# The router's logits of a fusion layer: weight columns as the stationary side of TensorE's products, or 128 tokens

## The chip, the core and the metric

The kernel runs on one core of a Trainium2 chip. A time is the device time of one execution in microseconds (us). TensorE (PE) multiplies, VectorE (DVE), ScalarE (ACT) and GpSimd (POOL) work elementwise, SyncE (SP) starts transfers. A TensorE product has a stationary side, which is loaded first (a record of its own, PEld), and a moving side, whose columns then stream past it; the result stands in PSUM with the stationary side's columns as its partitions and the moving side's columns as its elements.

## The reference, cut to what matters

Images are cut into patches and embedded, joined with text to 16 sequences of 69 tokens (1104 tokens of 256 values), and pass one attention layer. Then comes a mixture of experts; the router is the part that changes:

```
h = h + attention(layernorm(h))
x = layernorm(h)                                  # 1104 tokens x 256
shared = expert(x, shared_up, shared_down)        # every token, gelu(x @ up) @ down
probs = softmax(x @ router_w)                     # router_w: 256 x 8 experts
top_k_prob, top_k_idx = top_k(probs, 2)
out = h + shared + x + sum over the 2 experts of prob * expert(x)
```

## The kernel before, in words

Every engine has its own list of instructions, written out by hand in one block; they meet at semaphores. There is no scheduler: the order in the code is the order on the engine.

After attention the normalized tokens stand transposed in `hT_n` as two parts, a rounded high part and the low rest (fp32r each; a product of two such numbers is three products: high x high, high x low, low x high, `split_product`). `flat_transposes(g)` turns group g of 276 tokens (four sequences) into PSUM, ACT writes the high part (`flat_high`), DVE the low part (`flat_low`, semaphore `f_lo`).

The shared expert goes over all tokens in 24 steps n: three blocks of SN = 384 tokens times eight slices of 128 hidden values. `shared_up(n)` is six products of 384 columns, ACT takes the gelu twice (`shared_act`, `s_act`), DVE writes the low part (`shared_parts`, `s_lo`), `shared_down(n)` is nine products of 256 columns. `shared_up(n)` waits until `s_lo` has reached n - 1, that is until DVE has taken step n - 2.

Between these steps the router is woven in. TPAD = 1152 padded tokens are NT = 9 tiles of 128 or NSG = 3 blocks of 384; NE = 8 experts, KD = 2 slices of the 256 inputs. `router(q)` makes the logits of block q as 8 partitions x 384 in PSUM bank 7, ACT copies them to `lturn` (`logits_copy`), and when all three are there `router_turn` turns them tile by tile, so that tokens are partitions. All three blocks use the same piece of bank 7, so `router(1)` and `router(2)` wait for the copy before them. DVE then takes the maximum and subtracts it (`r_sub`), ACT takes the exponential, for which it loads another table and afterwards the gelu's again, and DVE goes on with a long chain of small operations (top two, ranks, places), at the end of which stands the table `dest` that says which rows belong to which expert tile. Its parts alternate on DVE with `shared_parts`, so that a late chain holds up the shared expert's steps: `shared_parts(6, 7)` stands behind the softmax's sum and product.

After the shared expert TensorE runs 25 expert tiles in a loop, GpSimd gathers rows, splits expert weights and adds the results to the output.

The line numbers of before that the rows use: L978 to L980 are `split_product` (router, shared_up, experts), L853 every transpose, L1028 `shared_down`, L774 `logits_copy`, L804 the exponential, L723 `flat_high`, L716 `flat_base`, L768 and L769 `shared_act`, L1370 `shared_parts`, L1378 `shared_end`, L1412 and L1413 the maximum and the subtraction, L1091 the sums over tiles that give ranks.

Of the kernel before, what the change touches and what calls it, by code (L numbers as in the profile page):

```python
# [13 lines left out]
P = 128  # L14
# [52 lines left out]
def fusion_layer(nc, patches, txt, cls_token, cls_pos, ln1_gb, tok_w, tok_bias, ln2_g, ln2_b,  # L67
# [5 lines left out]
    def sb(name, shape, dt=F32, where=ctx, side="left"):  # L73
        return where.enter_context(nc.sbuf_tensor(name, shape, dt, side=side))

    def sem(name):
        return ctx.enter_context(nc.semaphore(name))
# [5 lines left out]
    with ctx:  # L83
# [15 lines left out]
        additions = sb("additions", [1, TILES], I32)  # L99
        tend_int = sb("tend_int", [1, NE], I32)  # L100
        rw = sb("rw", [P, KD, NE])
        rws = sb("rws", [P, 2, KD, NE], F32R)
        st2 = sb("st2", [SEQ, NG, GB, 6])
        mv2 = sb("mv2", [SEQ, NG, GB, 2])
        rs2 = sb("rs2", [SEQ, NG, GB])
# [64 lines left out]
        slots12.close()  # L170

        sb("slots12", [P, 4 * EW], where=early)
        turned = ExitStack()
        lturn = sb("lturn", [NE, TPAD], where=turned)
        turned.close()
        in_lane = sb("in_lane", [P, 2 * NT, P], where=early)
        above = sb("above", [P, 2 * NT, TILES], where=early)
        in_tile = sb("in_tile", [P, 2 * NT, TILES], where=early)
# [45 lines left out]
        f_stats, f_rstd, f_normed, f_base, f_tr, f_hi, f_lo = (  # L224
            sem(n) for n in ("f_stats", "f_rstd", "f_normed", "f_base", "f_tr", "f_hi", "f_lo"))
        pads, rws_ready, logits = sem("pads"), sem("rws_ready"), sem("logits")
        l_turned, l_taken = sem("l_turned"), sem("l_taken")
        r_sub, r_exp, r_mask, r_prefix, r_tiles = (
            sem(n) for n in ("r_sub", "r_exp", "r_mask", "r_prefix", "r_tiles"))
        r_told, r_table_mm, r_table = sem("r_told"), sem("r_table_mm"), sem("r_table")  # L230
# [411 lines left out]
        def _(act):  # L642
# [126 lines left out]
                    nc.scalar.activation(up, up, ACT.Gelu).then_inc(s_act, 1)  # L769


            def logits_copy(q):
                act.wait_ge(l_turned, q + 1)
                nc.scalar.activation(lturn[:, SN * q:SN * (q + 1)], ps[0:NE, 7, 0:SN], ACT.Copy).then_inc(l_taken, 1)  # L774

            def expert_high(n):

                part, k = n // 4, n % 4
# [11 lines left out]
            flat_norm(2)  # L790
            shared_act(2, 3)
            flat_high(2)
            logits_copy(0)
            shared_act(3, 4)
            flat_norm(3)
            shared_act(4, 5)
# [1 line left out]
            shared_act(5, 6)  # L798
            flat_base(2)
            shared_act(6, 7)  # L800
            logits_copy(1)
            logits_copy(2)
            act.wait_ge(r_sub, 1)
            nc.scalar.activation(rout[:, 1, :], rout[:, 0, :], ACT.Exp).then_inc(r_exp, 1)  # L804
            shared_act(7, 8)
# [45 lines left out]
        def _(te):  # L851
            def transpose(o, i, n):
                return nc.tensor.transpose(o, i, ident[0:n, 0:n])  # L853
# [98 lines left out]
            def flat_transposes(g):  # L952
                te.wait_ge(f_normed, g + 1)
                te.wait_ge(a_rope, min(g + 3, NG))
                if g == 1:
                    te.wait_ge(f_lo, 1)
                elif g >= 2:
                    te.wait_ge(a_pTs, NG)
                    if g == 3:
                        te.wait_ge(f_lo, 3)  # L960
                for c in range(KD):
                    for b in range(GB):
                        last = transpose(flat_ps(g, c)[:, SEQ * b:SEQ * (b + 1)], hn2[:, g % 2, b, P * c:P * (c + 1)], SEQ)
                last.then_inc(f_tr, 1)
# [10 lines left out]
            def split_product(o, pairs):  # L975

                for n, (a, b) in enumerate(pairs):
                    nc.tensor.matmul(o, a[0], b[0], start=n == 0, stop=False)  # L978
                    nc.tensor.matmul(o, a[0], b[1], start=False, stop=False)  # L979
                    last = nc.tensor.matmul(o, a[1], b[0], start=False, stop=n == len(pairs) - 1)  # L980
                return last

            def router(q):

                te.wait_ge(a_exp, NG)
                te.wait_ge(rws_ready, 1)
                te.wait_ge(f_lo, GROUPS_OF[q])
                if q >= 1:
                    te.wait_ge(l_taken, q)
                split_product(ps[0:NE, 7, 0:SN],  # L990
                              [([rws[:, v, c, :] for v in range(2)],
                                [hT_n[:, v, c, SN * q:SN * (q + 1)] for v in range(2)])
                               for c in range(KD)]).then_inc(l_turned, 1)

            def router_turn():
                te.wait_ge(l_taken, NSG)
                for i in range(NT):
                    last = transpose(ps[:, 7, SN + NE * i:SN + NE * (i + 1)], lturn[:, P * i:P * (i + 1)], NE)
                last.then_inc(logits, 1)

            def shared_up(n0, n1):

# [29 lines left out]
            def shared_steps(n0, n1):  # L1032
                for n in range(n0, n1):
                    shared_up(n, n + 1)
                    shared_down(n - LAG, n - LAG + 1)
# [37 lines left out]
            attention_out(NG - 1)  # L1073
            shared_up(2, 4)
            flat_transposes(2)
            router(0)
            shared_down(0, 1)
            shared_steps(4, 6)
            flat_transposes(3)
            shared_steps(6, 7)  # L1080
            te.wait_ge(pads, 1)
            router(1)
            router(2)
            router_turn()
            shared_steps(7, 10)

            te.wait_ge(r_mask, 1)
# [76 lines left out]
        def _(dve):  # L1164
# [196 lines left out]
            v.tensor_scalar(token[:, :], small[:, S_TOK:S_TOK + NT], -float(T + P), None, ALU.add)  # L1361

            dve.wait_ge(router_in, 16)
            link(v.tensor_copy(rws[:, 0, :, :], rw[:, :, :]))
            v.tensor_tensor(rws[:, 1, :, :], rw[:, :, :], rws[:, 0, :, :].bitcast(F32), ALU.subtract).then_inc(rws_ready, 1)

            def shared_parts(n0, n1):
                for n in range(n0, n1):
# [39 lines left out]
            over_e = lambda a: a.unsqueeze(2).to_broadcast([P, NT, NE])  # L1408
            rank = small[:, S_RANK:S_RANK + NE].unsqueeze(1).to_broadcast([P, NT, NE])
            dve.wait_ge(logits, 1)  # L1410
            lg = n3(ps[:, 7, SN:SN + NT * NE])
            link(v.tensor_reduce(rsm[:, 0, :], lg, AX.X, ALU.max))  # L1412
            v.tensor_tensor(n3(rout[:, 0, :]), lg, over_e(rsm[:, 0, :]), ALU.subtract).then_inc(r_sub, 1)  # L1413
            dve.wait_ge(r_exp, 1)
            link(v.tensor_reduce(rsm[:, 1, :], n3(rout[:, 1, :]), AX.X, ALU.add))
            link(v.reciprocal(rsm[:, 2, :], rsm[:, 1, :]))
# [196 lines left out]
```

## Time and profile before

| | |
|---|---|
| median of 3 runs | 341.75 us (339.48 to 342.25) |
| the profiled execution's time | 340.2 us |
| its span in the profile | 338.4 us |
| mean granted TensorE clock | 0.984 of full speed |
| busy: PE, PEld, DVE, ACT, POOL | 89%, 80%, 47%, 43%, 62% |
| router, first product of block 0 to DVE's maximum | 92.72 to 107.17 us |
| shared expert's last product, expert tiles | to about 157 us, then to 330 us |

Times of single rows are microseconds from the span's start. A busy share says how long an engine had something in it, not that it set the end; the waits say that.

### The profile page before, as it was taken

How to read it: one execution, taken by the hardware profiler on the slowest of the kernel's cores; microseconds unless marked ns; L12 is line 12 of the kernel's file. 1: busy time of each engine (PE TensorE's matmuls, PEld its weight loads, DVE VectorE, ACT ScalarE, POOL GpSimd, SP SyncE). 2: the span in 40 equal slices, each digit the busy share in tenths (PEclk: the TensorE clock that was granted, in tenths of full speed). 3: DMA queues.
4: the chain of work that ended last, by engine and by line, in shares of the span. 5: the costliest groups of instructions: out<-in, count | busy, mean ns of one | idle time of the engine just before them, and what ended most of it. 6: DMA issues, size and time to landing. Idle time of an engine off the chain costs nothing.

```text
span 338.4 us, 6655 instructions
## 1 busy us (share of the span) xinstructions
PE 301.1 (89%) x2049; PEld 269.5 (80%) x2050; DVE 159.8 (47%) x402; ACT 145.3 (43%) x327; POOL 210.0 (62%) x168
## 2 busy tenths in 40 slices
PE   0879788998897969999899999999999999999970
PEld 0456587887795969998699989998999899899960
DVE  3558867888853399473223332433233233323220
ACT  2647313375978533642444344333433343344210
POOL 2476373148882000755988988898888899335551
PEclk9997979999999999999999999999999999999997
DMA  7955404002464230375453364255333633224522
GB/s 235 314 104 158 144 26 158 0 27 63 153 211 157 97 119 2 108 239 193 164 169 108 137 201 163 52 172 186 114 111 101 175 57 47 34 44 47 64 33 31
DMA packets 21926, 39.91 MB, mean 118 GB/s; under 512 B 2914, under 2 KB 18227, under 8 KB 19603
## 3 DMA queue, kind: packets, MB, share of 16 engines
q0 software_dynamic: 7456, 25.43, 28.0%
q1 hardware_dynamic: 14162, 14.03, 13.4%
q10 hardware_dynamic: 288, 0.20, 0.2%
q8 instruction: 11, 0.18, 0.2%
q14 instruction: 9, 0.07, 0.1%
HBM read 28.84 MB, written 6.93 MB: 106 GB/s over the span
## 4 chain that ended last, share of the span: by engine, by line
PE 41%; POOL 12%; DMA 12%; issue 8%; DVE 7%; ACT 2%; POOLq 2%; SPq 0%; DVEq 0%; ACTq 0%
DMA out_tokens<-xy_all,dest 11%; PE ps L978 9%; PE ps L979 9%; PE ps L980 9%; PE ps L1028 7%; POOL ring L443 6%; PE ps L853 4%; POOL ring L442 3%; POOL out_tokens L590 2%; PE ps L948 2%; POOLq L587 1%; PE ps L1100 1%; DVE h L1286 1%; DVE ps L1258 1%; DVE qk L1257 1%
## 5 line engine op out<-in xcount | busy, mean ns | idle before, releaser
L443 POOL TENSOR_TENSOR ring<-stage,ring 128x512 fp32r<-128x512 f32 (+2 forms) x30 | 76.2, 2541 | 2.5
L1549 DVE TENSOR_TENSOR hgT<-ps,hgT 128x512 fp32r<-128x512 f32 x50 | 32.2, 687 | 72.2 <-ACT hgT L843 72.2
L978 PE MATMUL ps<-ring,hgT 128*128 x200 | 58.0, 290 | 2.1 <-DVE xy_all L1555 1.5
L590 POOL DMA_INDIRECT out_tokens<-xy_all,dest x25 | 39.5, 1582 | 27.5 <-DMA out_tokens<-xy_all,dest 15.6
L980 PE MATMUL ps<-ring,hgT 128*128 x200 | 55.9, 279 | 0.0
L979 PE MATMUL ps<-ring,hgT 128*128 x200 | 55.9, 279 | 0.0
L835 ACT ACTIVATE hg<-ps 128x512 f32<-128x512 f32 x50 | 29.9, 599 | 47.6 <-PE ps L980 47.6
L580 POOL DMA_INDIRECT xy_all<-normalized_tokens,dest x25 | 24.9, 997 | 38.8 <-DVE dest L1511 31.4
L978 PE MATMUL ps<-ring,xgT 128*128 x100 | 41.3, 413 | 1.1 <-issue 0.6
L442 POOL TENSOR_SCALAR ring<-stage 128x512 fp32r<-128x512 f32 (+2 forms) x30 | 38.5, 1284 | 2.6 <-PEq L1114 2.4
L978 PEld LDWEIGHTS ps<-ring,hgT 128*128 128x128 f32 x200 | 37.6, 188 | 2.6 <-issue 2.6
L979 PE MATMUL ps<-ring,xgT 128*128 x100 | 39.4, 394 | 0.0
L980 PE MATMUL ps<-ring,xgT 128*128 x100 | 39.2, 392 | 0.0
L979 PEld LDWEIGHTS ps<-ring,hgT 128*128 128x128 f32 x200 | 37.7, 188 | 0.0
L980 PEld LDWEIGHTS ps<-ring,hgT 128*128 128x128 f32 x200 | 37.6, 188 | 0.0
L818 ACT ACTIVATE xgT<-ps 128x256 fp32r<-128x256 f32 x25 | 9.6, 386 | 53.7 <-PE ps L853 53.7
L1555 DVE TENSOR_SCALAR xy_all<-ps,gate 128x256 f32 (+1 forms) x25 | 12.1, 484 | 38.6 <-PE ps L980 38.6
L1028 PE MATMUL ps<-ring,hid 128*128 128x256 f32 x216 | 29.5, 282 | 0.2 <-DVE base L1378 0.2
L1028 PEld LDWEIGHTS ps<-ring,hid 128*128 128x128 f32 x216 | 28.3, 189 | 0.6 <-issue 0.5
L843 ACT ACTIVATE hgT<-ps 128x512 fp32r<-128x512 f32 x50 | 27.1, 599 | 2.6 <-PE ps L853 2.6
L853 PE MATMUL ps<-mats,hg 128*128 128x128 f32 x200 | 25.9, 272 | 0.0
L853 PEld LDWEIGHTS ps<-mats,hg 128*128 128x128 f32 x200 | 23.3, 140 | 3.2
(193 smaller groups left out, 591.0 us busy)
## 6 DMA issues: line engine op xcount, KB each, us to landing
stage<-in_w_up POOLq DMA_DIRECT2D x9, 1024.0 KB, 5.5
stage<-in_w_dn POOLq DMA_DIRECT2D x9, 1024.0 KB, 5.6
xg<-xy_all SPq DMA_DIRECT2D x25, 128.0 KB, 2.7
xp<-in_patches SPq DMA_DIRECT2D x4, 384.0 KB, 7.6
normalized_tokens<-hn SPq DMA_DIRECT2D x4, 276.0 KB
residual_tokens<-h SPq DMA_DIRECT2D x4, 276.0 KB
ring<-in_tok_w SPq DMA_DIRECT2D x1, 768.0 KB, 7.0
base<-residual_tokens SPq DMA_DIRECT2D x2, 384.0 KB, 4.1
```

The costliest lines, as they stand in the source:

```text
L442: link(nc.gpsimd.tensor_scalar(hi, stage[:, part, c0:c1], 1.0, 0.0, ALU.mult, ALU.add))
L443: return nc.gpsimd.tensor_tensor(lo, stage[:, part, c0:c1], hi.bitcast(F32), ALU.subtract)
L580: pool.indirect_dma_start(xy_all[:, t, :], None, xn_d, bass.IndirectOffsetOnAxis(ap=dest[:, t:t + 1].bitcast(U32), axis=0)).then_inc(rows_ ...
L590: pool.indirect_dma_start(out, bass.IndirectOffsetOnAxis(ap=dest[:, t:t + 1].bitcast(U32), axis=0), xy_all[:, t, :], None, compute_op=ALU. ...
L835: nc.scalar.activation(hg[:, 1 - c, 512 * half:512 * (half + 1)], ps[:, hidden_bank + half, :], ACT.Gelu).then_inc(e_act, 1)
L843: nc.scalar.activation(hgT[:, c, 0, 4 * half:4 * half + 4, :], ps[:, turned_bank + half, :].rearrange("p (k t) -> p k t", k=4), ACT.Copy). ...
L853: return nc.tensor.transpose(o, i, ident[0:n, 0:n])
L978: nc.tensor.matmul(o, a[0], b[0], start=n == 0, stop=False)
L979: nc.tensor.matmul(o, a[0], b[1], start=False, stop=False)
L980: last = nc.tensor.matmul(o, a[1], b[0], start=False, stop=n == len(pairs) - 1)
L1028: last = nc.tensor.matmul(ps[:, down_bank[j], 0:D], a[x], b[y], start=f == 0 and m == 0, stop=f == KF - 1 and m == 2)
L1549: v.tensor_tensor(hgT[:, c, 1, 4 * half:4 * half + 4, :], ps[:, turned_bank + half, :].rearrange("p (k t) -> p k t", k=4), hgT[:, c, 0, 4 ...
```

## The change

The router's products change sides. 128 tokens of `hT_n` are the stationary side and the router's weights the moving one: for each tile of 128 tokens and each of the two slices, the high part of the tokens meets 16 columns (8 of the weights' high part and 8 of their low part, which `rws` now holds side by side), and the low part of the tokens meets the 8 high columns and is added onto the first 8. The logits then have tokens as partitions at once: each tile has 16 values of its own in bank 7, the three copies on ACT, the nine turns on TensorE, `lturn` and the two semaphores between them are gone. DVE adds the two halves: it copies the second to `rout` and adds the first, and then takes the maximum and subtracts from there.

The products are also placed otherwise. Before, block 0 (384 tokens) stood after `flat_transposes(2)` and blocks 1 and 2 together after step 6. Now tiles 0 to 3 (512 tokens) stand after `flat_transposes(2)`, tiles 4 and 5 after `flat_transposes(3)`, and tiles 6 to 8 after step 6.

```diff
-        rws = sb("rws", [P, 2, KD, NE], F32R)
+        rws = sb("rws", [P, KD, 2, NE], F32R)
...
-            def logits_copy(q):
-                act.wait_ge(l_turned, q + 1)
-                nc.scalar.activation(lturn[:, SN * q:SN * (q + 1)], ps[0:NE, 7, 0:SN], ACT.Copy).then_inc(l_taken, 1)
...
             flat_high(2)
-            logits_copy(0)
             shared_act(3, 4)
...
             shared_act(6, 7)
-            logits_copy(1)
-            logits_copy(2)
             act.wait_ge(r_sub, 1)
...
-            def router(q):
+            def logits_of(i):
+                return ps[:, 7, 2 * NE * i:2 * NE * (i + 1)]
+
+            def router(i0, i1):
 
                 te.wait_ge(a_exp, NG)
                 te.wait_ge(rws_ready, 1)
-                te.wait_ge(f_lo, GROUPS_OF[q])
-                if q >= 1:
-                    te.wait_ge(l_taken, q)
-                split_product(ps[0:NE, 7, 0:SN],
-                              [([rws[:, v, c, :] for v in range(2)],
-                                [hT_n[:, v, c, SN * q:SN * (q + 1)] for v in range(2)])
-                               for c in range(KD)]).then_inc(l_turned, 1)
-
-            def router_turn():
-                te.wait_ge(l_taken, NSG)
-                for i in range(NT):
-                    last = transpose(ps[:, 7, SN + NE * i:SN + NE * (i + 1)], lturn[:, P * i:P * (i + 1)], NE)
-                last.then_inc(logits, 1)
+                te.wait_ge(f_lo, -(-min(P * i1, T) // GT))
+                for i in range(i0, i1):
+                    for c in range(KD):
+                        high, low = (hT_n[:, n, c, P * i:P * (i + 1)] for n in range(2))
+                        nc.tensor.matmul(logits_of(i), high, rws[:, c, :, :].rearrange("p v e -> p (v e)"), start=c == 0,
+                                         stop=False)
+                        last = nc.tensor.matmul(logits_of(i)[:, 0:NE], low, rws[:, c, 0, :], start=False, stop=c == KD - 1)
+                if i1 == NT:
+                    last.then_inc(logits, 1)
...
             flat_transposes(2)
-            router(0)
+            router(0, 4)
             shared_down(0, 1)
             shared_steps(4, 6)
             flat_transposes(3)
+            router(4, 6)
             shared_steps(6, 7)
             te.wait_ge(pads, 1)
-            router(1)
-            router(2)
-            router_turn()
+            router(6, NT)
             shared_steps(7, 10)
...
-            lg = n3(ps[:, 7, SN:SN + NT * NE])
-            link(v.tensor_reduce(rsm[:, 0, :], lg, AX.X, ALU.max))
-            v.tensor_tensor(n3(rout[:, 0, :]), lg, over_e(rsm[:, 0, :]), ALU.subtract).then_inc(r_sub, 1)
+            lg = ps[:, 7, 0:2 * NT * NE].rearrange("p (n v e) -> p n v e", v=2, e=NE)
+            link(v.tensor_copy(n3(rout[:, 1, :]), lg[:, :, 1, :]))
+            link(v.tensor_tensor(n3(rout[:, 0, :]), lg[:, :, 0, :], n3(rout[:, 1, :]), ALU.add))
+            link(v.tensor_reduce(rsm[:, 0, :], n3(rout[:, 0, :]), AX.X, ALU.max))
+            v.tensor_tensor(n3(rout[:, 0, :]), n3(rout[:, 0, :]), over_e(rsm[:, 0, :]), ALU.subtract).then_inc(r_sub, 1)
```

What stands on TensorE from `flat_transposes(3)` (the `hn` row) to `shared_up(7)` before; the `ring` rows are a shared step's products, the `rws` rows the router's. Left out are the rest of step 6 and of the router's twelve products:

```order
L853 MATMUL ps<-mats,hn 128x69 x8
L978 MATMUL ps<-hT_n,ring 128x384
...
L1028 MATMUL ps<-ring,hid 128x256 x9
L978 MATMUL ps<-hT_n,rws 8x384
L979 MATMUL ps<-hT_n,rws 8x384
L980 MATMUL ps<-hT_n,rws 8x384
...
L853 MATMUL ps<-mats,lturn 128x8 x9
L978 MATMUL ps<-hT_n,ring 128x384
```

And in the changed kernel, at the same place:

```order
L842 MATMUL ps<-mats,hn 128x69 x8
L983 MATMUL ps<-rws,hT_n 128x16
L985 MATMUL ps<-rws,hT_n 128x8
...
L967 MATMUL ps<-hT_n,ring 128x384
...
L1016 MATMUL ps<-ring,hid 128x256 x9
L983 MATMUL ps<-rws,hT_n 128x16
L985 MATMUL ps<-rws,hT_n 128x8
...
L967 MATMUL ps<-hT_n,ring 128x384
```

Eight short products now stand ahead of step 6 and twelve behind it, where twelve long ones and nine turns stood behind it.

On ACT, from `flat_high(3)` to the exponential, before:

```order
L723 ACTIVATE hT_n<-ps 128x276 x2
L768 ACTIVATE hid<-ps 128x384
L769 ACTIVATE ps<-ps 128x384
L716 ACTIVATE h<-h,nb,sp 69x256 x4
L768 ACTIVATE hid<-ps 128x384
L769 ACTIVATE ps<-ps 128x384
L774 ACTIVATE lturn<-ps 8x384 x2
L804 ACT_TABLE_LOAD
L804 ACTIVATE rout<-rout 128x72
```

And in the changed kernel:

```order
L719 ACTIVATE hT_n<-ps 128x276 x2
L764 ACTIVATE hid<-ps 128x384
L765 ACTIVATE ps<-ps 128x384
L712 ACTIVATE h<-h,nb,sp 69x256 x4
L764 ACTIVATE hid<-ps 128x384
L765 ACTIVATE ps<-ps 128x384
L793 ACT_TABLE_LOAD
L793 ACTIVATE rout<-rout 128x72
```

The two copies between the gelu of step 6 and the table load are gone; nothing else moved on ACT but the first copy, further up.

## Rows read from the trace of the kernel before

**Rows 1.** The page: busy time, share of the span and instructions of each engine.

```profile
PE 301.1 (89%) x2049; PEld 269.5 (80%) x2050; DVE 159.8 (47%) x402; ACT 145.3 (43%) x327; POOL 210.0 (62%) x168
```

**Rows 2.** The chain that ended last, in order of time: start us, us, what.

```profile
101.41 1.97 ACT h L716 x4
...
104.12 0.40 ACT lturn L774
...
118.93 0.75 DVE base L1378 x2
...
160.58 1.98 DMA xg<-xy_all
```

**Rows 3.** Timeline, 92 to 95 us: start us, us, engine line op [idle before <-releaser].

```profile
92.72 0.37 PE L978 MATMUL ps<-hT_n,rws 128*8 128x384 f32 x1
...
93.81 1.22 PE L1028 MATMUL ps<-ring,hid 128*128 128x256 f32 x9
...
94.25 0.55 DVE L1370 TENSOR_TENSOR hid<-ps,hid 128x384 fp32r<-128x384 f32 x1
...
94.94 0.42 PE L978 MATMUL ps<-hT_n,ring 128*128 128x384 f32 x1
```

**Rows 4.** Timeline, 99 to 107 us.

```profile
99.24 0.67 PE L853 MATMUL ps<-mats,hn 69*128 69x69 f32 x8
...
99.75 0.42 PE L978 MATMUL ps<-hT_n,ring 128*128 128x384 f32 x1
...
99.94 0.70 ACT L723 ACTIVATE hT_n<-ps 128x276 fp32r<-128x276 f32 x2 [0.93 <-PE ps L853]
...
100.88 1.23 PE L1028 MATMUL ps<-ring,hid 128*128 128x256 f32 x9
...
101.94 0.34 PE L978 MATMUL ps<-hT_n,rws 128*8 128x384 f32 x1
...
104.04 0.46 ACT L774 ACTIVATE lturn<-ps 8x384 f32<-8x384 f32 x1
...
104.65 0.33 PE L978 MATMUL ps<-hT_n,rws 128*8 128x384 f32 x1 [1.50 <-ACT lturn L774]
...
105.88 0.48 ACT L774 ACTIVATE lturn<-ps 8x384 f32<-8x384 f32 x1 [1.38 <-PE ps L980]
106.38 1.28 ACT L804 ACT_TABLE_LOAD   x1
```

**Rows 5.** Timeline, 107 to 110 us.

```profile
107.06 0.45 PE L978 MATMUL ps<-hT_n,ring 128*128 128x384 f32 x1
...
107.17 0.23 DVE L1412 TENSOR_REDUCE rsm<-ps 128x9 f32<-128x72 f32 x1 [5.18 <-PE ps L853]
...
107.44 0.23 DVE L1413 TENSOR_TENSOR rout<-ps,rsm 128x72 f32<-128x72 f32 x1
...
107.71 0.26 ACT L804 ACTIVATE rout<-rout 128x72 f32<-128x72 f32 x1
...
108.78 0.56 DVE L1370 TENSOR_TENSOR hid<-ps,hid 128x384 fp32r<-128x384 f32 x1
...
109.48 0.42 PE L978 MATMUL ps<-hT_n,ring 128*128 128x384 f32 x1
```

**Rows 6.** Weight loads in the timeline from 113.5 us.

```profile
113.93 2.09 PEld L1091 LDWEIGHTS ps<-rsel,mats 128*128 128x128 f32 x18
115.94 0.30 PEld L1094 LDWEIGHTS ps<-mats 128*128 128x128 f32 x2
```

**Rows 7.** One tile's instructions (lturn): ns min/median/max, first and last start us.

```profile
L853 PEld LDWEIGHTS ps<-mats,lturn x9: 133/137/138, 106.4 to 106.9; 8*128 8x128 f32 x9
L853 PE MATMUL ps<-mats,lturn x9: 200/201/223, 106.4 to 106.9; 8*128 8x8 f32 x9
```

**Rows 8.** GpSimd's timeline from 112 us.

```profile
135.97 1.07 POOL L580 DMA_INDIRECT xy_all<-normalized_tokens,dest  x1 [31.41 <-DVE dest L1511]
...
330.78 1.56 POOL L590 DMA_INDIRECT out_tokens<-xy_all,dest  x1 [1.17 <-DVE xy_all L1555]
```

More of the change, by code:

```diff
@@ L172, in fusion_layer @@
         sb("slots12", [P, 4 * EW], where=early)
-        turned = ExitStack()
-        lturn = sb("lturn", [NE, TPAD], where=turned)
-        turned.close()
         in_lane = sb("in_lane", [P, 2 * NT, P], where=early)
@@ L226, in fusion_layer @@
         pads, rws_ready, logits = sem("pads"), sem("rws_ready"), sem("logits")
-        l_turned, l_taken = sem("l_turned"), sem("l_taken")
         r_sub, r_exp, r_mask, r_prefix, r_tiles = (
@@ L1363, in _ @@
             dve.wait_ge(router_in, 16)
-            link(v.tensor_copy(rws[:, 0, :, :], rw[:, :, :]))
-            v.tensor_tensor(rws[:, 1, :, :], rw[:, :, :], rws[:, 0, :, :].bitcast(F32), ALU.subtract).then_inc(rws_ready, 1)
+            link(v.tensor_copy(rws[:, :, 0, :], rw[:, :, :]))
+            v.tensor_tensor(rws[:, :, 1, :], rw[:, :, :], rws[:, :, 0, :].bitcast(F32), ALU.subtract).then_inc(rws_ready, 1)
             def shared_parts(n0, n1):
```

## The prediction

> **What bounds the kernel now.** I began with the page: TensorE has something in it for 89% of the span, the others for 43 to 62% [rows 1]. That alone says little about the router, so I followed the chain of work that ended last through it [rows 2]. It is on TensorE nearly everywhere, but between 100 and 107 us it leaves it: it runs through ACT's `flat_base` and gelu and then through a copy to `lturn`. The reader is to see in [rows 4] that this is a ping-pong: copy of block 1 on ACT at 104.04, block 2's products on TensorE at 104.65 after 1.50 us of idleness, copy of block 2 on ACT at 105.88, and right behind it the load of the exponential's table, 1.28 us. DVE waits 5.18 us for the logits and starts at 107.17, the exponential at 107.71 [rows 5].
>
> Who waits for that? The shared step 6 on DVE stands behind the softmax; it runs from 108.78 to 109.34, and TensorE's `shared_up(8)` starts at 109.48, 0.14 us after it [rows 5]. From there the chain goes on through TensorE, DVE's `shared_end`, and the first rows for the expert tiles [rows 2]. GpSimd sits idle for 31.41 us until the table `dest` comes out of the same DVE chain, and its last addition waits for DVE's last result [rows 8]. I found nothing behind 109.48 that is due at a fixed time, so a shift there should reach the end whole.
>
> **What the change removes.** From the start of the first late copy to the start of the table load, 104.04 to 106.38, there are 2.34 us on ACT [rows 4]: two copies, block 2's products between them and the waits. All of it goes. The nine turns go too. The copy of block 0 lies in a stretch where ACT afterwards waits anyway; I count nothing for it.
>
> **What one new product costs.** It loads 128 columns and moves 16 or 8. No router product of before is like that: they load 8 columns and move 384, at 1.09 us for six with what lies around them (92.72 to 93.81) [rows 3]. The nearest row is L1091: 128 columns loaded, 8 to 72 moved, and 18 loads go from 113.93 to the next group's at 115.94, 2.01 us or 0.112 us each [rows 6]. The load sets this pace, since the moved columns change and the pace doesn't. The lower end is the nine turns of `lturn`, also 128 columns loaded and 8 moved, whose starts lie within 0.5 us, 0.064 us each [rows 7]. They are turns, though, and a load there lasts 137 ns where L1094's two take 0.30 us together [rows 6, 7]. I take 0.112.
>
> The Trainium skill, "TensorE: Matmul & The Clock Gate", section "Back-to-back issue gap", gives about 81 ns for a sustained pair of load and product at 128 columns. L1091 of this case doesn't agree, with 112 ns. By the page the delay ahead of `flat_transposes(3)` below would be 0.14 us and the gain 2.2 us, an estimate of 338.0 us for the profiled execution.
>
> **What the change adds, place by place.** Tiles 0 to 3 are 16 products, 1.79 us where 1.09 stood. `shared_down(0)` is nine products, 1.06 us (as from 100.88 to 101.94 [rows 4]), so it ends at 92.72 + 1.79 + 1.06 = 95.57. `shared_up(4)` starts at 94.94 now, just behind DVE's step 2 (94.25 + 0.55 = 94.80) [rows 3]. TensorE is therefore 0.63 us late there, and no wait up to `flat_transposes(3)` takes it back, as the two steps between run without a gap. So this delay is on the path: the turns start at 99.24 + 0.63 = 99.87, and ACT, which waits for them (0.93 us before L723 [rows 4]), is late by the same 0.63.
>
> On ACT the rest up to the table load is unbroken work: the load starts at 104.04 + 0.63 = 104.67 and ends at 105.95 instead of 107.66.
>
> On TensorE: 99.87 + 0.51 (the turns, 99.24 to 99.75) + 8 x 0.112 + 1.13 (`shared_up(6)`, 99.75 to 100.88) + 1.06 + 12 x 0.112 = 104.81 [rows 4, 6]. ACT's `flat_base` hides the 0.90 us of tiles 4 and 5 from ACT's path; without that cover they would cost it 0.90 more. With the last product's own length (0.20, as in [rows 7], less the pace) DVE can start at about 104.95.
>
> DVE has two more operations ahead of the maximum, a copy and an addition of 128 x 72. The two that are there follow each other by 0.27 us and last 0.23 each [rows 5]: four make 3 x 0.27 + 0.23 = 1.04 us, 0.54 more than now. The difference is ready at 104.95 + 1.04 = 105.99, where it was at 107.67. It comes within 0.04 us of the table load, so both paths give the same. The exponential starts at about 106.03 instead of 107.71: **1.7 us earlier**.
>
> What is late next? DVE's step 6 ends at 109.34 - 1.7 = 107.66, and `shared_up(8)` can start at 107.8. TensorE arrives at 104.81 + 1.13 + 1.06 = 107.0, so it stands idle for 0.8 us. `shared_up(7)` is 2.25 us earlier (107.06 to 104.81 [rows 5]), but 0.6 of that is given back here. Work added to TensorE on balance: 36 x 0.112 = 4.0 us against 18 products at 1.09 us for six and nine turns at 0.064, 3.9 us. It is the waiting that goes, not the work.
>
> **The sum.** The profiled execution's 340.2 us less 1.7 is 338.5. It lies 1.55 us under the median of the three runs; on that scale the forecast is 341.75 - 1.65 = **340.1 us**, half a per cent faster. The three runs spread over 2.8 us, so a change of less than about 1% is what a measurement of this kernel can hardly tell from none.
>
> **Rivals.**
>
> *The new products are cheap* (0.064 us, the turns' pace). Then tiles 0 to 3 take 1.02 us and delay nothing, the table load starts at 104.04, the exponential at 104.04 + 1.28 + 0.04 = 105.36, and the gain is 2.35 us: 339.4 on the median's scale. DVE would be ready before, so ACT's path sets it. For it speaks that the turns have the same columns on both sides, against it that they are no arithmetic. Were TensorE the bound behind the router, the gain would be 2.25 us, nearly the same; the 0.14 us between DVE's step 6 and `shared_up(8)` speaks against that.
>
> *The time is taken back later*: some transfer or GpSimd's additions set the rest, and nothing changes, 341.75. For it: GpSimd is busy for 62% of the span [rows 1] and additions to the output follow one another. Against it: the last addition waits for DVE's last result and not for the addition before it [rows 8], and GpSimd's gathers start when DVE says so.
>
> *The new products are dear*: slower. The products of before on `hT_n` and `rws` are one record each, with 384 columns moved [rows 3]; L1091's nine are recorded as eighteen, two passes with a load each [rows 6]. No row shows the router's type with 16 columns. Should it take two passes, a product costs 0.224 us. Tiles 0 to 3 then take 3.58 us, the delay ahead of `flat_transposes(3)` is 2.42 us, and DVE's difference is ready at 99.24 + 2.42 + 0.51 + 8 x 0.224 + 1.13 + 1.06 + 12 x 0.224 + 0.14 + 1.04 = 110.02, 2.35 us later than now: 344.1. With c for one product, that time is 101.96 + 36 c; it decides at c = 0.159 us. Four passes would cost 10 us, which I hold for hardly possible.
>
> **How the numbers follow.** The forecast has 0.68, the cheap products 0.16, time taken back 0.09, dear products 0.07 (0.01 of it four passes). Each case's median is uncertain by about 1.3 us, half of the spread of the runs. The range 338.2 to 342.4 takes in the cheap case and most of the case of no change, and leaves out the dear one. Faster by over 1% would need 3.4 us, more than any case has, so only scatter gives it: 0.06. Slower by over 1% needs four passes, or two and scatter: 0.04. Within 1%: 0.90.
>
> **What would show it.** Starts of the router's weight loads 0.11 us apart, one record each; `flat_transposes(3)` some 0.6 us later against the work ahead of it; the table load right behind step 6's gelu, and the exponential about 13.3 us after the router's first product instead of 15.0; a gap of 0.8 us on TensorE before `shared_up(8)`; then every later landmark, DVE's `dest` and the last addition, earlier by the same 1.7. The prediction is wrong if the loads stand at 0.06 or above 0.16 us, or if a landmark behind `shared_up(8)` doesn't move with it.

## The result, and the profile after

Over 22 runs each, the changed kernel has a median of 339.35 us against 341.11 us before; the ratio is 0.9933, with a 95% interval of 0.9911 to 0.9955. The ratio and its interval leave out every execution that took over 1.5% more than the fastest of its own kernel, two of before (345.66 and 347.63 us) and six of the changed kernel (five of 342.1 to 342.6 us at a granted clock of 0.970 and one of 1048.85 us that nothing here explains), so that the 2.3 us (1.5 to 3.0) it stands for are more than the 1.76 us between the two medians. With the one of 1048.85 us alone left out, the medians lie 1.8 us apart and the means 2.0. The forecast was 1.65 us, ratio 0.9952, a median of 340.1 us. The profiled execution took 339.25 us with a span of 337.4 us, against 340.2 and 338.4 us: 0.95 us less, where 1.7 was forecast for it (338.5).

The two profiled executions reach the router 0.76 us apart (first router product at 92.72 and at 93.48 us), though nothing ahead of it was changed. So I compare distances from one point ahead of it: the start of the turns of the last attention probabilities on TensorE, 87.29 us before and 88.01 us after. I call them landmarks. (In the profiles of all the kernels below that point itself lies anywhere from 85.52 to 89.78 us.)

| from that point, us | before | after | difference |
|---|---|---|---|
| turns of `flat_transposes(3)` | 11.95 | 12.62 | +0.67 |
| load of the exponential's table | 19.09 | 17.52 | -1.57 |
| exponential | 20.42 | 18.81 | -1.61 |
| first gathered rows (`dest` is ready) | 48.68 | 47.04 | -1.64 |
| first addition to the output | 110.03 | 108.39 | -1.64 |
| last addition to the output | 243.49 | 241.82 | -1.67 |

Two later profiles, of the changed kernel once more and of before with one alteration far behind the router (the wide table, below), repeat this: 18.85 and 20.52 us at the exponential, 47.06 and 48.76 at the first gathered rows, 243.05 and 244.77 at the last addition, which is 1.7 us each time.

The router's products in the changed kernel, as the instructions of one tile (`rws`): ns min/median/max, then first and last start in us.

```profile
L983 PEld LDWEIGHTS ps<-rws,hT_n x18: 188/192/192, 93.5 to 105.2; 128*128 128x128 f32 x18
L983 PE MATMUL ps<-rws,hT_n x18: 170/256/256, 93.5 to 105.2; 128*128 128x16 f32 x18
L985 PEld LDWEIGHTS ps<-rws,hT_n x18: 187/192/192, 93.6 to 105.3; 128*128 128x128 f32 x18
L985 PE MATMUL ps<-rws,hT_n x18: 252/253/253, 93.6 to 105.3; 128*128 128x8 f32 x18
```

Eighteen of each: one record per product, so the router's type makes a single pass at 16 and 8 columns too. The record's own length (0.25 us) isn't the pace, since one product starts before the one ahead of it has ended. The pace is read from the timeline between the first product and what follows the sixteenth:

```profile
93.01 0.67 PE L842 MATMUL ps<-mats,hn 69*128 69x69 f32 x8
93.48 0.26 PE L983 MATMUL ps<-rws,hT_n 128*128 128x16 f32 x1
93.59 0.25 PE L985 MATMUL ps<-rws,hT_n 128*128 128x8 f32 x1
...
95.27 1.31 PE L1016 MATMUL ps<-ring,hid 128*128 128x256 f32 x9
```

From 93.48 to 95.27 are 16 products in 1.79 us, 0.112 us each, as L1091 had it [rows 6] and not as the turns had it [rows 7].

The chain that ended last, between the turns and `shared_up(8)`; start us, us, what. It answers to the piece in [rows 2] that went through two copies to `lturn`:

```profile
100.79 0.52 PE ps L842 x8
...
101.63 0.40 ACT hT_n L719
102.03 0.38 ACT hid L764
102.41 0.38 ACT ps L765
102.79 1.97 ACT h L712 x4
104.76 0.37 ACT hid L764
105.14 0.37 ACT ps L765
...
105.53 1.19 ACT L793
...
106.82 0.27 ACT rout L793
...
107.89 0.57 DVE hid L1357
...
108.60 0.41 PE ps L967
```

ACT now works without a break from the turns to the end of the table load. DVE's side of it, from the timeline of DVE; it answers to [rows 5]:

```profile
105.63 0.23 DVE L1399 COPY rout<-ps 128x72 f32<-128x72 f32 x1 [2.25 <-PE ps L985]
105.90 0.23 DVE L1400 TENSOR_TENSOR rout<-ps,rout 128x72 f32<-128x72 f32 x1
106.16 0.23 DVE L1401 TENSOR_REDUCE rsm<-rout 128x9 f32<-128x72 f32 x1
106.43 0.23 DVE L1402 TENSOR_TENSOR rout<-rout,rsm 128x72 f32<-128x72 f32 x1
107.11 0.23 DVE L1404 TENSOR_REDUCE rsm<-rout 128x9 f32<-128x72 f32 x1 [0.45 <-ACT rout L793]
```

The difference is ready at 106.66, the table at 106.81: the two paths end 0.15 us apart, ACT's last. The wait for the logits is 2.25 us where it was 5.18 us. TensorE's timeline shows the idle time that was to appear before `shared_up(8)`:

```profile
108.60 0.41 PE L967 MATMUL ps<-hT_n,ring 128*128 128x384 f32 x1 [0.79 <-DVE hid L1357]
```

And GpSimd's timeline answers to [rows 8]:

```profile
135.05 1.07 POOL L576 DMA_INDIRECT xy_all<-normalized_tokens,dest  x1 [29.78 <-DVE dest L1500]
...
329.83 1.56 POOL L586 DMA_INDIRECT out_tokens<-xy_all,dest  x1 [1.59 <-DVE xy_all L1544]
```

### The profile page after: what moved, and what is told of

Its sections match the earlier page's. It is cut to its first block, busy times and chain, and to the rows that moved or that the text cites. A ratio compares the mean times of both kernels' runs of the same rounds, so it can differ in the third digit from the quotient of the medians.

```text
span 337.4 us, 6671 instructions
## 1 busy us (share of the span) xinstructions
PE 301.1 (89%) x2058; PEld 271.4 (80%) x2059; DVE 160.3 (48%) x404; ACT 144.0 (43%) x324; POOL 210.9 (63%) x168
## 4 chain that ended last, share of the span: by engine, by line
PE 42%; POOL 13%; DMA 11%; issue 9%; DVE 6%; ACT 3%; POOLq 3%; SPq 0%; DVEq 0%; ACTq 0%
DMA out_tokens<-xy_all,dest 10%; PE ps L967 9%; PE ps L969 9%; PE ps L968 9%; PE ps L1016 6%; POOL ring L439 6%; PE ps L842 4%; POOL ring L438 3%; POOL out_tokens L586 3%; POOLq L583 2%; PE ps L937 2%; PE ps L1087 1%; DVE h L1273 1%; PE ps L920 1%; DVE base L1365 1%
```

## The experiments

The theory: what was gained is the ping-pong between TensorE and ACT. After the change the exponential waits for two paths of nearly equal length, ACT's (whose one new term is the delay ahead of `flat_transposes(3)`) and TensorE's 36 loads at 0.112 us with DVE's four operations behind them. Rivals: the form of the products matters in itself; the early places matter; extra work on TensorE would be hidden.

**The old form, block 1 early.** Products, copies and turns as before; only block 1's place and its copy's differ.

```diff
             flat_transposes(3)
+            router(1)
             shared_steps(6, 7)
             te.wait_ge(pads, 1)
-            router(1)
             router(2)
...
             shared_act(5, 6)
+            logits_copy(1)
             flat_base(2)
             shared_act(6, 7)
-            logits_copy(1)
             logits_copy(2)
```

> The kernel before, with one thing moved: block 1 of the old router (8 weight columns loaded, 384 tokens moved) goes right behind flat_transposes(3), and its copy on ACT ahead of flat_base(2). Copies and turns stay. Landmark: from the start of the last attention probabilities' turns on TensorE to the exponential of the router's softmax; 20.42 us before, 18.81 us in the changed kernel. My theory (what was gained is the ping-pong of copies between TensorE and ACT): block 2 no longer waits, its copy starts behind step 6's gelu, the table load ends at about 106.2 and DVE's difference at 106.3 of before's scale, so the landmark is about 19.05 us, 1.35 us less than before and 0.25 us more than the changed kernel: about 0.4% faster than before. Rival (the gain needs the other form of the products): the landmark stays at 20.2 to 20.4 us and the time within 0.1% of before.

The landmark of the exponential is 19.04 us, the first gathered rows come at 47.29 us, 1.39 us sooner than before. The rows of its timeline show why: block 2 no longer follows a copy, and its own copy stands at the table load.

```profile
103.89 0.47 ACT L774 ACTIVATE lturn<-ps 8x384 f32<-8x384 f32 x1
104.26 2.06 ACT L716 ACTIVATE h<-h,nb,sp 69x256 f32<-69x256 f32 x4
...
105.50 0.34 PE L978 MATMUL ps<-hT_n,rws 128*8 128x384 f32 x1
...
107.01 0.47 ACT L774 ACTIVATE lturn<-ps 8x384 f32<-8x384 f32 x1
107.49 1.28 ACT L804 ACT_TABLE_LOAD   x1
```

So six sevenths of the gain at the exponential (1.38 of 1.61 us) are to be had without turning the products round. The rival falls. The 0.4% that was expected in the whole time doesn't show: the ratio is 1.0007 (0.9945 to 1.0069), too wide to tell. In its profile the granted clock is at half for 3.5 us at the end of the table's products (18 in two passes each, which make the table of rows), from 46.1 us after the reference point, and the last addition comes at 243.67 us. That is no sooner than in the first profile of before (243.49), but 1.1 us sooner than in the later one (244.77). The two differ in one stretch, from the first gathered rows to the first addition (61.35 and 62.54 us, last section); this run has 62.87 there, so the later one is the fairer comparison.

**The new form in the old places.** Tiles 0 to 2, then tiles 3 to 8 together.

```diff
-            router(0, 4)
+            router(0, 3)
...
-            router(4, 6)
             shared_steps(6, 7)
             te.wait_ge(pads, 1)
-            router(6, NT)
+            router(3, NT)
```

> The changed kernel with the router's tiles in the places of before: tiles 0 to 2 behind flat_transposes(2), tiles 3 to 8 together behind step 6. Landmark as in the other runs (turns of the last probabilities to the exponential; 18.81 us in the changed kernel). My theory: TensorE's sum of work ahead of the logits stays the same, 36 products at 0.112 us, and ACT's path is 0.45 us shorter, so the logits are ready at the same time and the landmark is 18.7 us (18.6 to 18.8). Rival (the early places bring part of the gain, since six products more stand ahead of the logits): the six products of 0.9 us show, landmark 19.7 us, and the gain over before falls by half.

The landmark is 18.72 us, as the sum of work has it, and the table load comes at 17.10, 0.42 us sooner than in the changed kernel. For the exponential the places are indifferent. But the first gathered rows come at 48.34 us, 1.3 us later than in the changed kernel. The busy times by stretch show the first part of what stands between. The columns are PE, PEld, DVE, ACT and POOL busy, the granted clock, the DMA engines' share and GB/s:

```profile
102.00:104.00 2.00, 2.00 (x21) 2.00 (x19) 0.24 (x1) 2.00 (x6) 1.32 (x3) 1.00 0.20 71
104.00:106.00 2.00, 2.00 (x14) 2.00 (x15) 0.93 (x4) 1.65 (x3) 0.56 (x1) 0.88 0.47 101
106.00:108.00 2.00, 2.00 (x11) 2.00 (x10) 1.58 (x6) 1.97 (x4) 0.00 (x0) 0.50 0.82 277
108.00:110.00 2.00, 2.00 (x12) 2.00 (x12) 1.79 (x8) 2.00 (x6) 0.00 (x0) 0.77 0.61 237
```

TensorE is busy all the time, and yet its clock falls to 0.50, which is 1.2 GHz instead of 2.4, from 105.5 to 109.0 us, 0.8 us behind the 24 router products in a row (102.03 to 104.74 us). A `shared_down` then has a load record of 2.15 us for its nine loads where 1.19 is usual. This part is 0.55 us: the table's products start 42.50 us after the reference point, and at 41.95 in the changed kernel. The rest comes in these products, during which the clock falls a second time. The changed kernel's, then this run's:

```profile
129.96 4.22 PE L1087 MATMUL ps<-told,in_lane 128*128 128x50 f32 x36
```

```profile
129.77 5.18 PE L1086 MATMUL ps<-told,in_lane 128*128 128x50 f32 x36
```

That second fall isn't a matter of the places: the next run but one has it with the router as in the changed kernel. And the profiled execution is one of the longer ones, 342.23 us at a granted clock of 0.966. Of the six, three have 0.966 and the others 0.979, 0.984 and 0.989, the last as high as in profiles with no fall (0.988), so the fall behind the 24 products need not be in every execution. Ratio 0.9925 (0.9849 to 1.0002).

**The router's products twice.** Each tile's four products are made into a spare piece of bank 7 first.

```diff
+                    for o in (spare_of(i), logits_of(i)):
-                    for c in range(KD):
+                        for c in range(KD):
```

> The changed kernel with every router product made twice, the first time into a piece of PSUM that nobody reads: 72 short products instead of 36, in the same places. This is the dear case of the prediction, made on purpose. By its sum (101.96 + 36 c with c = 0.224 us on before's scale) the exponential comes at 110.06, the landmark (turns of the last probabilities to the exponential) is 22.8 us, 4.0 us more than in the changed kernel, and the whole is 2.35 us slower than before, 0.7%. Rival (TensorE has idle time there that takes the extra work, 0.8 us before shared_up(8) and the waits further on): landmark below 22 us, or the end later by less than 1.5 us against before.

Ratio 1.0252 (1.0178 to 1.0326), 8.6 us slower than before: neither the sum nor the rival. The landmark is 24.24 us instead of 22.8. The router's products kept their pace (0.112 us apart in all three places), so the sum's terms are right; what came on top up to the exponential, 1.4 us, goes with a fall of the clock. Two stretches of the profile, the first with the 32 products in a row of the first place, the second behind them:

```profile
93.00:97.00 4.00, 4.00 (x41) 4.00 (x40) 3.93 (x15) 2.14 (x7) 2.59 (x5) 1.00 0.66 214
...
98.00:101.00 3.00, 3.00 (x13) 3.00 (x12) 0.00 (x0) 1.62 (x4) 2.83 (x4) 0.50 0.48 165
```

It fell to half from 97.9 to 101.4 us, again from 111.6 to 115.0 us behind the 24 products of the third place, and once more from 138.9 us, within the table's 36 products, for 6.9 us. The first gathered rows come 5.2 us later than before and the last addition 7.7 us. About 1.2 of the 2.5 us between these two are also found without any fall (last section), so not all of the loss is the clock's.

**One sum instead of copy and addition on DVE.**

```diff
-            link(v.tensor_copy(n3(rout[:, 1, :]), lg[:, :, 1, :]))
-            link(v.tensor_tensor(n3(rout[:, 0, :]), lg[:, :, 0, :], n3(rout[:, 1, :]), ALU.add))
+            link(v.tensor_reduce(n3(rout[:, 0, :]), lg.rearrange("p n v e -> p n e v"), AX.X, ALU.add))
```

> The changed kernel with DVE's copy and addition of the two halves of the logits replaced by one sum over the two (a reduction of 72 pairs). DVE's difference is then ready 0.2 to 0.27 us sooner. My theory: ACT's table load is the later one of the two in the changed kernel (it ends at 106.81 us, the difference at 106.66), so the exponential doesn't move: landmark 18.8 us (within 0.05), time unchanged. Rival (DVE's added operations are on the path): landmark 18.55 us. A reduction that reads pairs 8 apart could cost more than the 0.23 us of a plain one; up to 0.5 us it would still not show.

Landmark 18.77 us against 18.81, ratio 0.9942 (0.9871 to 1.0013). The two paths in its timeline:

```profile
103.16 1.28 ACT L793 ACT_TABLE_LOAD   x1
103.26 0.31 DVE L1399 TENSOR_REDUCE rout<-ps 128x72 f32<-128x144 f32 x1 [2.25 <-PE ps L985]
103.87 0.23 DVE L1401 TENSOR_TENSOR rout<-rout,rsm 128x72 f32<-128x72 f32 x1
104.45 0.26 ACT L793 ACTIVATE rout<-rout 128x72 f32<-128x72 f32 x1
```

DVE needs 0.84 us from the logits to the difference instead of 1.03, and the exponential follows the table load as before. DVE's added operations cost nothing in the changed kernel, because ACT's path is the longer one. The first gathered rows come at 47.71 us all the same, 0.67 us later than in the changed kernel: the clock is at half from 45.0 to 51.9 us after the reference point, and the table's products take 5.12 us instead of 4.22.

**ACT's `flat_base(2)` behind the softmax.**

```diff
             shared_act(5, 6)
-            flat_base(2)
             shared_act(6, 7)
...
             shared_act(7, 8)
+            flat_base(2)
             flat_base(3)
```

> The changed kernel with ACT's flat_base(2) (2.0 us, ahead of step 6's gelu and the table load) moved behind the softmax, just before flat_base(3). By the sum DVE's difference is the next one due, 0.15 us before the table load's end in the changed kernel's profile: the exponential gains 0.1 us (landmark 18.7) and no more. The price: the residual rows of group 2 leave 4 us later, group 3's behind them, and ACT's weight splitting, which waits for these transfers (1.6 us in the changed kernel), waits 3 us or more longer; step 8's gelu is 2 us later, which DVE's chain hides. I expect the first gathered rows on GpSimd (47.04 us after the turns of the last probabilities) within 0.3 us of that, and the whole 0 to 3 us slower than the changed kernel. Rival (flat_base is what holds the softmax, as the chain of waits has it for 2 us): landmark 17.0 to 17.5, 1.5 us faster than the changed kernel.

The mirror of the run above: the table load moves to 16.24 us, 1.28 us sooner, and the exponential stands at 18.71 us. ACT's timeline shows the new wait and the price:

```profile
104.42 1.28 ACT L792 ACT_TABLE_LOAD   x1
106.89 0.27 ACT L792 ACTIVATE rout<-rout 128x72 f32<-128x72 f32 x1 [1.19 <-DVE rout L1402]
...
124.83 0.63 ACT L776 ACTIVATE ring<-stage 128x512 fp32r<-128x512 f32 x1 [3.17 <-DMA residual_tokens<-h]
```

ACT waits 1.19 us for DVE ahead of the exponential, and later 3.17 us for the residual rows, where the changed kernel waits 1.64; half of the price that was expected, and the first gathered rows aren't later (46.95 us). Ratio 0.9948 (0.9918 to 0.9979), not to be told from the changed kernel's. The chain of waits had named `flat_base` with 2 us; taking all of it away gave 0.1. The rival falls, and the two runs together show that the two paths tie.

**One tile early, two tiles early.** TensorE waits 0.59 us for DVE ahead of the last `attention_out`. Tile 0, or tiles 0 and 1, go there, with one sum on DVE.

```diff
             attention_probs(NG - 1)
+            router(0, 1)
             attention_out(NG - 1)
...
-            router(0, 4)
+            router(1, 4)
```

> The changed kernel with tile 0 of the router (four products) ahead of the last attention_out, where TensorE waits 0.59 us for DVE, and with one sum instead of copy and addition on DVE. By the sum, tiles 1 to 3 now cost 1.34 us behind flat_transposes(2), so flat_transposes(3) is late by 0.18 us instead of 0.63, ACT's path is 0.45 us shorter and DVE's 0.45 + 0.25 us: the exponential comes 0.45 us sooner, landmark (turns of the last probabilities to the exponential) 18.35 us against 18.81. Everything behind shifts by the same 0.45. Rival (the wait for DVE is not free: the products delay attention_out): landmark 18.6 to 18.8 us. In the time that is 0.1%, below what the runs can tell.

> The same with tiles 0 and 1 early (eight products, 0.90 us in a wait of 0.59). TensorE is then 0.3 us late with attention_out, of which 0.27 us is taken back at shared_up(2), where it waits anyway, and tiles 2 and 3 cost 0.90 us where 1.16 us are free: no delay ahead of flat_transposes(3), landmark 18.2 us (18.15 to 18.35). Rival (attention_out is on the path to flat_norm(3) through DVE): the second tile gives nothing or costs 0.3 us, landmark 18.4 to 18.7.

With one tile the landmark is 18.39 us and the first gathered rows come at 46.65, 0.4 us sooner than in the changed kernel; ratio 0.9905 (0.9873 to 0.9937). With two it is 18.20 us, as the sum said, and 46.43; ratio 0.993 (0.9901 to 0.9959). The wait was free: the four products take the place of most of it, and `attention_out` follows after a rest of 0.20 us. With eight products there is no rest, and it starts 0.1 us later than in the changed kernel. The timeline with one tile:

```profile
85.52 0.44 PE L842 MATMUL ps<-mats,pr 69*69 69x69 f32 x4
85.77 0.26 PE L983 MATMUL ps<-rws,hT_n 128*128 128x16 f32 x1
...
86.55 1.95 PE L937 MATMUL ps<-vv,prT 69*69 69x256 f32 x8 [0.20 <-DVE prT L1265]
```

**Wide products against the falling clock.** Two runs were to test whether few moved columns make the clock fall. In one the table's 18 products move 100 columns instead of 50, in the other the added 36 router products move 128 columns instead of 16 or 8.

```diff
+                m = min(n + 2, 2 * NT)
-                last = nc.tensor.matmul(ps[:, 6, TABLE:TABLE + 2 * TILES], in_lane[0:r, n, :],
-                                        told[0:r, n, :, :].rearrange("p a t -> p (a t)"),
+                last = nc.tensor.matmul(ps[:, 6, TABLE:TABLE + 2 * TILES * (m - n)], in_lane[0:r, n, :],
+                                        told[0:r, n:m, :, :].rearrange("p n a t -> p (n a t)"),
```

> The changed kernel with one thing different behind the router: the 18 products that make the table of rows (two passes each, 36 loads at 0.117 us) move 100 columns instead of 50, the second 50 being the next product's, whose sums go to a piece of PSUM that nobody reads. In three of the four experiments so far the granted clock fell to half right after these products, for 2 to 4 us, and in the changed kernel's profile it did not. Theory C (long runs of products that load 128 columns and move few make the clock fall): with more columns moved in the same time the clock stays at full speed behind the table, the distance from the first gathered rows on GpSimd to its first addition stays at 61.3 us as in the two kernels' profiles (62.9 to 63.7 us where the clock fell), and the median lies 1 to 2 us below the changed kernel's, ratio to before 0.988 to 0.990. Rival (the fall has to do with something else, or is a matter of the run): clocks of single runs scatter from 0.97 to 0.99 as in the changed kernel, ratio 0.993. The table's products themselves last 4.2 us in both theories, since loads set their pace; if moved columns did, 1.5 us more.

> As the run with the router's products made twice (72 products, each with its own load of 128 columns), but the added 36 move 128 columns each instead of 16 or 8, into a piece of PSUM that nobody reads. Theory C (thin products make the clock fall, and this made that run 8 to 9 us slower than before instead of the 2.35 us of the sum): the loads keep their pace of 0.112 us, the clock stays full at and after the router, the landmark (turns of the last probabilities to the exponential) is 22.8 us as the sum has it, not 24.2, and the whole is 2.0 to 3.5 us slower than before, ratio 1.006 to 1.012. Rival (the 72 loads themselves, or the PSUM traffic, slow the engine): landmark 24 us or more and ratio about 1.025 again, or more, since more is moved.

The wide table: 339.18 us, ratio 0.9931 (0.9895 to 0.9967), landmark 18.82, no fall in its profile. The gain of 1 to 2 us over the changed kernel that theory C expected (ratio 0.988 to 0.990) isn't there. The distance from the gathered rows to the first addition is 62.6 us all the same and not 61.3, so that distance doesn't measure the clock alone (below). The wide router products: ratio 1.0121 (1.0039 to 1.0203), but the six executions run from 343.18 to 350.35 us with a median of 348.77, against 349.94 with the narrow ones, so a smaller loss isn't shown; and the landmark is 25.8 us, later still. The profiled execution is one of the longest, 350.19 us. The stretches show a fall while the 32 products of the first place still run:

```profile
94.00:97.00 3.00, 3.00 (x31) 2.92 (x30) 2.90 (x13) 2.48 (x7) 1.68 (x3) 1.00 0.47 113
97.00:104.00 7.00, 7.00 (x35) 7.00 (x35) 1.76 (x5) 2.86 (x6) 6.75 (x8) 0.56 0.58 223
...
111.00:115.00 4.00, 4.00 (x35) 4.00 (x34) 0.74 (x4) 2.08 (x4) 0.00 (x0) 1.00 0.17 53
```

The third place had none this time. So the theory that few columns are the cause is not borne out: with products of 128 moved columns among them one fall stayed away and the other didn't. Within the table's products or at their end, 6 of the 11 profiles with the narrow products have a fall (all four of the first set, where the expectation above counted three) and none of the 3 with the wide ones, which is too few to call it shown.

**Both together, the kernel before with the wide table, and the changed kernel again**, on one chip.

> The changed kernel once more, on the chip and beside the runs of the three that follow. Open is why the measured gain (2.3 us, ratio 0.9933) is larger than the 1.6 to 1.7 us by which every landmark of its profile moved. Theory 1: the rest is the clock; single runs of before have more and deeper falls than those of the changed kernel (lowest granted clocks 0.952 to 0.962 against 0.970), so the runs at the highest clock of either kernel differ by 1.7 us and the medians by more. Theory 2: it is scatter; another set gives a ratio nearer 0.9955. Expected: landmark (turns of the last probabilities to the exponential) 18.8 us again, ratio 0.990 to 0.996, median of the runs' clocks 0.98 or higher and above before's by about 0.003.

> The best one so far (tile 0 early, one sum on DVE) with the table's products 100 columns wide. If wide products keep the clock up behind the table, no run has a clock below 0.985 but for other causes, and the median is 337.5 to 338.3 us, ratio 0.987 to 0.990. If they don't matter: the scatter of clocks from 0.980 to 0.989 and the ratio 0.9905 of the run with tile 0 early. Landmark 18.39 us as there.

> The kernel before with only the table's 18 products widened from 50 to 100 moved columns. It has the old router. If thin products of the table (36 loads in a row) are what lowers the clock in single runs, the clocks of its runs lie above those of before on the same chip (median 0.984 or more against 0.975 to 0.982) and it is 1 to 2 us faster, ratio 0.994 to 0.997. If the falls come from elsewhere (the attention, the waits around the router, the loop's end), nothing changes: ratio 1.000 within 0.3%.

The changed kernel again: 339.47 us, ratio 0.9941 (0.9902 to 0.998), landmark 18.85, first gathered rows 47.06. Both theories allowed such a ratio (0.990 to 0.996), so it doesn't decide between clock and scatter. One tile early with the wide table: 338.21 us, 0.9889 (0.9848 to 0.9931), landmarks 18.39 and 46.63, the lowest median of all. Before with the wide table: 341.74 us, ratio 1.000 (0.9965 to 1.0036). There no effect of the table's width shows, within 0.4%, and its gain in the other is not shown. By the intervals the best kernels aren't told from the changed one; by the landmark they are 0.4 us ahead.

## Why the prediction was right

**The bound**: right. The ping-pong was on the path, and the run with the old form and one block placed early takes most of the gain at the exponential (1.38 of 1.61 us) and at the first gathered rows (1.39 of 1.64) without any other change.

**One product's cost**: 0.112 us taken from L1091, 0.112 measured over 16. The turns' 64 ns don't hold here. They too load 128 columns and move 8, but a turn's load record lasts 133 to 138 ns, and those of L1091 and of the new products 187 to 192: the row with a load of the same kind, for arithmetic, was the one to choose. The 81 ns of the Trainium skill, "TensorE: Matmul & The Clock Gate", section "Back-to-back issue gap", which it gives for a sustained pair that moves 128 columns, don't hold here either, with 112 ns for pairs that move 16 or 8.

**The delay ahead of `flat_transposes(3)`**: 0.63 us said, 0.67 measured (12.62 against 11.95).

**The two paths**: the difference on DVE was to be ready 13.27 us after the router's first product, the table load to end after 13.23; measured are 13.18 and 13.33. The order within the tie came out the other way round. The exponential comes 13.34 us after the router's first product where 13.31 was said, and that product comes 0.04 us later after the reference point (5.47 against 5.43): together the step from 1.68 to 1.61. That it is a tie is shown by two runs, each of which shortens one path (0.19 us on DVE, 1.28 us on ACT) and moves the exponential by 0.04 and 0.10; a second profile of the changed kernel itself differs by 0.04.

**What is late next**: idle time of 0.8 us before `shared_up(8)` said, 0.79 measured.

**That the shift reaches the end whole**: 1.64 us at the gathered rows, 1.67 at the last addition, and 1.70 and 1.72 in the second pair of profiles.

**The rivals.** Cheap products: excluded by the pace. Time taken back: excluded by the landmarks. Dear products: a single pass, so it didn't arise; but its price was wrong. The sum gave 2.35 us over before for twice the work, and it measured 8.6 us. The working of that rival has no term for the clock, which wasn't at full speed, so its break-even at 0.159 us per product may be too kind. The forecast itself was spared since runs of 16, 8 and 12 products left the clock at full speed near the router in both profiles of the changed kernel.

**The size**: the median lies 0.75 us below the forecast one, inside the range, and most of that is the starting point: over 22 executions before itself has a median of 341.11 us, 0.64 less than the 341.75 of three on which the forecast was built. From 341.11 the forecast gain of 1.65 us leads to 339.46, measured are 339.35. That it comes so near is luck in part, with single executions of before spread over 338.9 to 347.6 us; the landmarks, with 1.61 to 1.72 us, are the firmer evidence. The ratio's 2.3 us is 0.6 more than the landmarks have. Part of that comes from the executions that it leaves out, as told at the top. Part may be the granted clock: beside the last set of experiments six of 29 executions of before lie at 0.962 or below and none of 12 of the changed kernel below 0.970, while those at 0.985 or more have medians of 340.4 and 338.5 us, 1.9 us apart. Whether the old router lowers the clock in single executions, with its waits and its nine small turns, stays open: the profile of before shows no such fall.

## What to carry to other kernels

Where two engines hand a buffer back and forth, first look whether one of the hand-overs can be made earlier in the work that stands around it: it gave 1.38 of 1.61 us at the exponential here. When such a wait goes, write down both paths that meet behind it; if they tie, as here, an improvement of one alone gives next to nothing (0.04 and 0.10 us). Price a product with few moved columns by a row whose load is of the same kind and length. Look at the granted clock where many of them stand in a row: 24 and more were followed by a fall here, 16 weren't. And compare profiles by distances from a point ahead of the change.

## What the runs showed of the hardware

The granted clock fell while TensorE was busy without a gap. After 24 products in a row that each load 128 columns and move 16 or 8 (2.7 us) it went from 2.4 to 1.2 GHz for 3.5 us, in the two profiles that have this, and after 32 of them (3.6 us) likewise in one, each time 0.8 to 1.1 us after the last of them; after 16, 12 and 8 it stayed at full speed near the router in all five profiles with these places, and in the three with a tile or two placed earlier. Adding products of 128 moved columns among them didn't keep it up reliably. What the deciding quantity is, the runs don't show.

Profiles of one and the same kernel differ in the distance from the first gathered rows to the first addition: 61.35 us in the first profile of the changed kernel, 62.57 in the second, with the clock at full speed in both. The first profile of before has 61.35 too, and none of the other eleven is below 62.5: the five without a fall lie at 62.54 to 62.61, the six with one at 62.87 to 63.76. The second of the changed kernel has DVE's `shared_end` start late; in DVE's timeline of the two, first then second:

```profile
142.74 1.08 DVE L1365 TENSOR_TENSOR base<-base,ps 128x256 f32<-128x256 f32 x3 [1.11 <-PE ps L1016]
```

```profile
141.86 0.42 DVE L1365 TENSOR_TENSOR base<-base,ps 128x256 f32<-128x256 f32 x1 [2.35 <-PE ps L1016]
```

ACT is late by 0.8 us at the same place, and TensorE, named as the releaser, isn't. What holds the two engines up was not found. It is worth 1.2 us, nearly three quarters of the whole change, so behind it only profiles of the same kind can be compared: the first of before with the first of the changed kernel, and the two later ones with each other.
